# Attention's even half: the output projection one slot later, the third part of the values one slot earlier

## The reference

```
def _L0_xattn_ref(x, context, Wq, Wk, Wv, Wout, bout):
    q, k, v = x @ Wq, context @ Wk, context @ Wv      # 8 heads of 64
    attn = softmax(q k^T * 64 ** -0.5)
    out = (attn v), heads side by side, 512 wide
    return out @ Wout + bout
x = x + _L0_xattn_ref(_layernorm(x), ctx_768, Wq, Wk, Wv, Wout, bout)
x = x + _L0_ffn_ref(_layernorm(x), ...)
```

## Time and profile before

| what | value |
|---|---|
| median of 3 runs | 1315.21 us (1313.83 to 1321.61) |
| profiled execution | 1315.97 us, of which its span is 1314.2 us |
| PE busy | 1171.0 us, 89% |
| PE weight loads busy | 1048.1 us, 80% |
| DVE busy | 862.4 us, 66% |
| POOL busy | 802.0 us, 61% |
| ACT busy | 767.5 us, 58% |

### The profile page before, as it was taken

The page is one execution under the profiler, slowest core; times in us unless marked ns, Lnnn a source line. Parts: engine busy times, 40 slices in busy tenths (PEclk is TensorE's granted clock), DMA queues, the critical chain, the costliest instruction groups (busy, mean ns, idle before and its releaser), DMA issues. The chain is left out here.

```text
span 1314.2 us, 27203 instructions
## 1 busy us (share of the span) xinstructions
PE 1171.0 (89%) x7454; PEld 1048.1 (80%) x7454; DVE 862.4 (66%) x2309; ACT 767.5 (58%) x1967; POOL 802.0 (61%) x867
## 2 busy tenths in 40 slices
PE   4889999989998999999899769997898999999892
PEld 3788888888888888888888658786787888888682
DVE  4878888888888888888888836665443333333230
ACT  4778788778877887887788433331133433433240
POOL 3778777977887787778778725564214444443341
PEclk9989999999999999999999879988899999999896
DMA  4203232222213131322222256221345335335634
GB/s 124 80 20 107 60 105 78 86 80 97 86 50 116 69 109 54 108 75 98 68 97 95 80 184 233 81 72 72 109 138 140 59 59 146 60 59 151 225 54 128
DMA packets 77104, 128.46 MB, mean 98 GB/s; under 512 B 18817, under 2 KB 63697, under 8 KB 72881
## 3 DMA queue, kind: packets, MB, share of 16 engines
q1 hardware_dynamic: 62256, 102.80, 23.1%
q0 software_dynamic: 14784, 24.84, 9.4%
HBM read 77.81 MB, written 53.48 MB: 100 GB/s over the span
## 5 line engine op out<-in xcount | busy, mean ns | idle before, releaser
L513 POOL TENSOR_TENSOR probs<-probs,inv_sum 112x375 f32<-112x375 f32 x256 | 208.9, 817 | 137.7 <-DVE inv_sum L762 137.5
L607 ACT ACTIVATE probs<-bank,neg_max 112x375 f32<-112x375 f32 x256 | 147.3, 575 | 131.8 <-DVE neg_max L750 129.4
L1203 POOL DMA_INDIRECT z_scratch<-stage,to_row x63 | 100.8, 1599 | 199.1 <-DMA z_scratch<-stage,to_row 105.2
L1449 DVE TENSOR_TENSOR hT_lo<-bank,hT_hi 128x512 fp32r<-128x512 f32 x91 | 62.9, 691 | 242.4 <-ACT hT_hi L1247 232.4
L1241 ACT ACTIVATE stage<-bank 128x512 f32<-128x512 f32 x91 | 54.4, 598 | 157.5 <-PE bank L1513 142.5
L699 DVE TENSOR_TENSOR keys<-bank,keys 64x376 fp32r<-64x376 f32 x256 | 140.1, 547 | 7.0
L750 DVE TENSOR_REDUCE neg_max<-bank 112x1 f32<-112x375 f32 x256 | 137.9, 539 | 8.8 <-PE bank L816 8.8
L777 DVE TENSOR_TENSOR pT_lo<-bank,pT_hi 125x336 fp32r<-125x336 f32 x256 | 129.8, 507 | 17.2 <-ACT pT_hi L622 11.2
L924 PE MATMUL bank<-ident,probs 112*125 112x112 f32 x768 | 127.3, 275 | 7.0 <-POOL probs L513 6.9
L924 PEld LDWEIGHTS bank<-ident,probs 112*125 112x125 f32 x768 | 119.7, 192 | 16.2 <-POOL probs L513 14.0
L816 PE MATMUL bank<-pT_hi,v_hi 125*128 125x224 f32 x384 | 112.5, 293 | 21.7 <-DVE pT_lo L777 19.9
(11 more groups left out here) (262 smaller groups left out, 3502.2 us busy)
## 6 DMA issues: line engine op xcount, KB each, us to landing
w_split_scratch<-stage SPq DMA_DIRECT2D x16, 1536.0 KB, 5.6
ring<-w_split_scratch SPq DMA_DIRECT2D x16, 1536.0 KB
stage<-in_L_ffn_W SPq DMA_DIRECT2D x48, 256.0 KB, 3.2
ctx_in<-in_ctx SPq DMA_DIRECT2D x32, 281.2 KB
xg<-x_sorted_scratch POOLq DMA_DIRECT2D x63, 136.0 KB, 3.5
x_in<-in_x SPq DMA_DIRECT2D x16, 224.0 KB, 4.1
x_res<-in_x SPq DMA_DIRECT2D x32, 112.0 KB, 2.7
x_scratch<-x SPq DMA_DIRECT2D x32, 112.0 KB, 2.0
```

The lines of the kernel that those rows point to most:

```text
L513: pool.tensor_tensor(probs[:, s % 4, :], probs[:, s % 4, :], inv_sum[:, s:s + 1].to_broadcast([N, M]), ALU.mult).then_inc(probs_ready, 1)
L607: act.activation(probs[:, s % 4, :], S_BANK[s % 2][0:N, 0:M], ACT.Exp, bias=neg_max[:, s:s + 1], accum_out=row_sum[:, s:s + 1]).then_inc(e ...
L1203: pool.indirect_dma_start(out=z_dram[:, :], out_offset=bass.IndirectOffsetOnAxis(ap=to_row[:, j:j + 1], axis=0), in_=y_sb[j % 3], in_offse ...
```

## The change

In the list of the even half, `wout` goes from slot 4 to slot 5 (the fifth and sixth slot), and `v2` from slot 5 to slot 4. Everything that follows the list moves with them: TensorE's matmuls, ScalarE's copy and GpSimd's two instructions for `v2`, VectorE's residual for `wout` (from its slot 5 to its slot 6, ahead of the low part of `xt0`), SyncE's store behind it, and the bank that each takes. No instruction is added or taken away, and the order within the lists is otherwise as it was.

```
-        ([], ["wout"]), ([], ["v2", "xt0"]), ([], ["xt1"]), ([], ["v1", "k3"])]
+        ([], ["v2"]), ([], ["wout", "xt0"]), ([], ["xt1"]), ([], ["v1", "k3"])]
```

## The result

The change makes the kernel slower: 1341.87 us median of 4 runs (1339.11 to 1344.17) against 1314.52 us (1313.16 to 1321.61) for the kernel before, a ratio of 1.0196 with a 95% interval of 1.0154 to 1.0238. The prediction was 1342 us. The profiled execution took 1342.79 us, its span is 1341.0 us, 26.8 us more than before.

A forecast was written before the change was run, and what follows sets the result against it. DVE's stretch without a wait up to the end of `xn` was taken to bound the pass. Pair 0 0.97, loop 14 x 0.90 = 12.6 and clock 8 x 1.7 = 13.6 gave 27.2 us more, 1342.4 us; range 1315 to 1354.

The forecast's parts named there:

- What bounds the pass: Slots 4 to 6: DVE sets the time up to the end of `xn`, then DVE and ACT in turn, then PE.
- The signs named beforehand: Profile after: `xn`'s second instruction near 1.85 us, DVE waits about 0.8 and 0, pairs of 45.9 or 47.6 us.
- The wait removed on PE: PE's 1.09 us wait for `oT_lo` ahead of `wout` goes, but a later wait for `pT_lo` remains; value 0.
- The delay at xn: On DVE, `xn`'s second instruction must also let POOL's `v_hi` pass, so `xn` ends 0.97 us later per pass.
- The first rival: DVE's `xn` gets in before POOL's `v_hi`, so the change does nothing: 1315 to 1318 us, chance 0.17.
- The residual: Leaving DVE's slot 5 wins 0 to 0.14 us, 0.07 taken; in slot 6 it fits a wait, 0 lost.
- The clock: PE's gathered pauses lower the granted clock to 0.50 for 3.40 us, costing 1.7 us; 8 falls taken, bounds 0 and 14.
- One premise: PE's new stretch around the wait for `xn` holds 1.2 to 1.6 us of work in 4 us, emptier than both compared.
- The total: Pair 0 0.97, loop 12.6 and clock 13.6 us, together 27.2 us over the median of 1315.21: 1342.4 us.
- Weight loads: The last load lands at 422.67, POOL's split wants it at 422.70: a tie, value 0, at most 1.0 us in one pass.
- The rival on the other side: PE's wait of 1.09 us is really won in each pass: 15.3 us less, 1299.9 us, chance 0.04.

The follow-up runs named there:

- a_wout_only: Against the kernel before, only `wout` moves, to slot 5 ahead of `v2`, which stays in slot 5; 1324.23 us, ratio 1.0175.
- h_v2_before_probs: The whole change, but POOL makes `v_hi` and `v_lo` of `v2` ahead of its multiplication of slot 4; 1307.54 us, one run.
- g_xn_in_gap_v2_early: The change with `xn` moved into DVE's slot 5 behind `neg_max`, `xt0` and `xt1` both in slot 6; 1338.81 us, ratio 1.0215 of the kernel before.
- k_change_again: The change itself, unaltered, measured again on another chip against the kernel before; 1325.91 us, ratio 1.0205.

## Why the prediction was right

- *What bounds the pass*: right. The signs named beforehand came: `xn`'s second instruction at 1.89 us (1.85 said), DVE's waits at 0.73 and 0 (0.8 and 0), passes of 45.83 and 47.43 us (45.9 and 47.6). The wait removed on PE came back as 0.25 + 1.07 us, and nothing was won there. That DVE's stretch up to the end of `xn` sets the pass is shown from both sides: 0.99 us more at `xn` made a pass 1.01 us longer than with POOL's part put back, and taking `xn` out of the stretch made it up to 1.17 us shorter.
- *The delay at xn*: predicted 0.97 us, measured 2.25 - 1.27 = 0.98. It is shown to be POOL's doing by the run that moved POOL's two instructions alone. The first rival, DVE ahead of `v_hi` by the order of issue, is refuted in all 15 places of the change, and in all 86 such places of the 13 traces. The rule of the Trainium skill ("SBUF — State Buffer", section "Who interferes with whom") that the first to issue goes first does not hold at this boundary: the second `xn` instruction starts in the trace at 332.35 - 1.89 = 330.46, 0.70 us ahead of `v_hi` (331.16), and ends 0.16 us behind it. At the end of `v_lo` the trace agrees with the rule: the first `xn` instruction, started at 330.10, 0.24 us ahead of the multiplication (330.34), ends at 330.53, while the multiplication has 0.67 us to go.
- *The residual*: 0.07 us taken, 0.16 measured, which is above the bound of 0.14; so a pass grew by 1.01 - 0.16 = 0.85 us and not by 0.90. Its place in slot 6 cost nothing, as said, but only because `v2` stands ahead of `wout` in the list: the bank of `xt1` was not among my steps, and a_wout_only shows that it would have cost as much as the delay at `xn`.
- *The clock*: 8 falls of 1.7 us taken, 6 of 1.60 in the loop and two falls' worth in pair 0. That the clock would fall, and the price, were worked out from rows; the count was a choice between 0 and 14. One premise failed: the new stretch was to hold 1.2 to 1.6 us of work in 4 us, less than either of the two rows it was set beside (1.90 and 1.83). In the trace PE's stretch from the wait for `xn` to the product is 3.38 us long (331.41 to 334.79), not 3.8 to 4.2, and from the loop's second pass on the emptiest four microseconds hold 1.92 to 1.96 us of work, in passes with a fall and without.
- *The total was luck in part.* Loop: 12.6 us said, 11.9 measured; clock: 13.6 said, 9.6 in the loop; pair 0 and ahead of it: 0.97 said, 3.1 measured; expert stage: in no term, 2.4 measured. The falls were put 4.0 us too high, and the 4.5 us that pair 0 and the expert stage brought in excess made up for it. Pair 0's 2.65 us can be put together, as an estimate, from 0.97 for `xn`, 3.4 for its 6.8 us at 1.2 GHz, and 1.7 less because a later stretch at 1.2 GHz lasted 10.2 us before (from 81.6) and 6.8 in the change (from 86.8).
- *Weight loads*: the tie held. POOL waited for them in three of the passes, 0.60, 0.33 and 0.22 us, and no pass is longer for it.
- *The rival on the other side*, 1299.9 us: refuted, as the second wait on PE said.

## What to carry to other kernels

Before work is moved into another engine's idle time, look which instruction of a third engine runs best in that idle time: here POOL's pause of 1.58 us was what kept a VectorE instruction short that lay on the path. In a hand-made order, test a half of a change only with the resources of the whole: which bank a unit waits for went with the order of the names, and each half alone cost 1% to 2% for a reason of its own. And where PE's pauses are gathered in one place, price the clock as well as the wait.

## What the runs showed of the hardware

A VectorE `tensor_scalar` with both operands in SBUF (0.41 us for 112x256 when POOL is idle, 0.80 us for a pair in single passes of two runs) did not end while the POOL instruction under which it began was running; it ended 0.15 us after a POOL instruction's end, in all 358 cases of the 13 traces. At the end of `v_lo`, or of its counterpart for the weights (L494), it was let in, with the next POOL instruction already under way, in all the 13 traces, and at the end of `v_hi` in h_v2_before_probs. But where it began under POOL's multiplication and the next POOL instruction followed at once, it had to wait for that one too: in pair 15 of the kernel before twice, in the change in all 15 places, in g_xn_in_gap_v2_early in its first instruction, and in 86 of 86 places of the 13 traces. What makes the multiplication's end different from the others is not settled.

The same chain of waits gave the clock different fates from pass to pass: of fourteen passes with the same order of work, six had a fall (3.4 us each, one of 6.8 in k_change_again) and eight kept the grant, in two profiles, three of the six in other passes. PE's two pauses in that stretch are 1.05 to 1.08 and 0.97 to 1.00 us long in every pass but the first. In the pass from 375.94 the fall stands at 380.38, in the pass from 423.26 at 428.16; the last two rows below are a pass with the fall at its end and one that kept the grant:

```profile
376.38:380.38 4.00, 2.18 (x17) 1.00 0.00 0
424.16:428.16 4.00, 1.93 (x14) 1.00 0.00 0
331.02:335.02 4.00, 1.97 (x15) 1.00 0.00 0
```

So how busy PE was just ahead does not tell by itself which pass falls; why one does and the next does not stays open.
